# Two-layer decoder on one core: the causal mask of the transposed scores moves from mask matmuls on TensorE to a GpSimd selection on the exponentials

## The reference, cut to what matters

```
qkv = x @ W_qkv;  q = layernorm(q, q_scale);  k = layernorm(k, k_scale)
scores = einsum("bshd,bthd->bhst", q / sqrt(8), k)
scores = where(future, finfo.min, scores)          # keys behind the query are left out
attn   = softmax(scores);  ctx = einsum("bhst,bthd->bshd", attn, v)
x = layernorm(x + ctx @ W_out)
```

## Time and profile before

| | |
|---|---|
| three runs | 491.47, 491.82, 494.59 us; median 491.82 |
| profiled execution | 493.74 us, its span in the trace 491.9 us |
| PE | 458.1 us busy, 93% |
| DVE | 384.5 us, 78% |
| ACT | 351.2 us, 71% |
| POOL | 190.2 us, 39% |
| mean granted clock of TensorE | 0.984 |

### The profile page before, as it was taken

The page is one execution under the profiler, slowest core; times in us unless marked ns, Lnnn a source line. Parts: engine busy times, 40 slices in busy tenths (PEclk is TensorE's granted clock), DMA queues, the critical chain, the costliest instruction groups (busy, mean ns, idle before and its releaser), DMA issues.

```text
span 491.9 us, 12390 instructions
## 1 busy us (share of the span) xinstructions
PE 458.1 (93%) x4416; PEld 307.2 (62%) x4416; DVE 384.5 (78%) x1133; ACT 351.2 (71%) x893; POOL 190.2 (39%) x365
## 2 busy tenths in 40 slices
PE   5567989998999999999999999999999999999994
PEld 2344557655546546666778555658754756996894
DVE  3559998799899999997788888858788678554465
ACT  3326676866858769887776688986767878969743
POOL 8760001570101644344143232334414537646352
PEclk9689999999999999999999999999999999999999
DMA  7650310032300213001110000030000000000001
GB/s 240 152 148 4 105 31 25 4 86 73 88 4 23 66 39 85 17 2 26 35 35 21 6 3 2 4 88 4 2 13 13 0 2 1 1 2 1 1 1 43
DMA packets 27185, 18.40 MB, mean 37 GB/s; under 512 B 8217, under 2 KB 26773, under 8 KB 26997
## 3 DMA queue, kind: packets, MB, share of 16 engines
q1 hardware_dynamic: 23413, 15.44, 11.8%
q10 hardware_dynamic: 3712, 2.17, 1.7%
HBM read 5.58 MB, written 1.05 MB: 13 GB/s over the span
## 4 chain that ended last, share of the span: by engine, by line
PE 74%; DVE 9%; POOL 6%; issue 3%; ACT 3%; DMA 2%; SPq 2%; ACTq 0%; POOLq 0%; DVEq 0%
PE psum L1051 11%; PE psum L1372 6%; PE psum L1162 6%; PE psum L1395 6%; PE psum L1308 6%; PE psum L1103 5%; PE psum L1130 4%; DVE nmax L1788 4%; PE psum L1406 4%; PE psum L1152 3%; PE psum L1149 3%; PE psum L1417 2%; PE psum L1190 2%; PE psum L1082 2%; PE psum L1109 1%
## 5 line engine op out<-in xcount | busy, mean ns | idle before, releaser
L1537 ACT ACTIVATE EX<-psum 128x1024 f32<-128x1024 f32 (+1 forms) x128 | 118.5, 976 | 8.7 <-PE psum L1136 4.3
L1788 DVE TENSOR_REDUCE nmax<-psum 128x2 f32<-128x768 f32 (+1 forms) x96 | 77.5, 861 | 7.4 <-PE psum L1109 7.2
L1783 DVE TENSOR_REDUCE nmax<-psum 128x4 f32<-128x616 f32 (+1 forms) x80 | 68.1, 876 | 2.9 <-PE psum L1103 2.6
L1103 PE MATMUL psum<-K,Q 64*128 64x154 bf16 (+4 forms) x512 | 50.9, 268 | 5.9 <-issue 4.5
L1014 POOL TENSOR_TENSOR GP<-REST,xrs 128x512 f32<-128x512 f32 (+1 forms) x48 | 32.5, 700 | 41.4 <-DVE xrs L2025 27.6
L1130 PE MATMUL psum<-Q,K 64*128 64x512 bf16 (+3 forms) x320 | 44.7, 315 | 1.6 <-DVE nmax L1788 1.2
L1620 ACT ACTIVATE REST<-psum,nxmax 128x154 f32<-128x154 f32 x96 | 36.2, 395 | 10.7 <-DVE nxmax L2015 9.8
L1444 ACT COPY pvraw<-psum 128x512 f32<-128x512 f32 x32 | 18.7, 585 | 34.3 <-PE psum L1162 24.6
L1103 PEld LDWEIGHTS psum<-K,Q 64*128 64x128 bf16 x512 | 21.4, 95 | 28.2 <-issue 19.1
L1162 PE MATMUL psum<-EX,V 128*32 128x256 f32 (+3 forms) x512 | 37.8, 435 | 0.1
L945 POOL TENSOR_SCALAR rstd_rest<-moments_rest 128x2 f32<-128x2 f32 x32 | 7.3, 228 | 79.1 <-DVE moments_rest L1831 78.7
(11 more groups left out here) (338 smaller groups left out, 1162.4 us busy)
## 6 DMA issues: line engine op xcount, KB each, us to landing
Q<-xparts SPq DMA_DIRECT2D x24, 128.0 KB
Q<-parts SPq DMA_DIRECT2D x21, 128.0 KB
K<-parts SPq DMA_DIRECT2D x21, 128.0 KB
X<-in_x SPq DMA_DIRECT2D x4, 256.0 KB, 3.6
Q<-in_L_xattn_Wkv SPq DMA_DIRECT2D x1, 1024.0 KB, 6.6
K<-xkparts SPq DMA_DIRECT2D x24, 38.5 KB
out<-XB_rest SPq DMA_DIRECT2D x6, 128.0 KB, 1.9
Q<-in_L_xattn_Wq SPq DMA_DIRECT2D x1, 512.0 KB, 4.4
```

The costliest lines, as they stand in the source:

```text
L1103: last = mm(to[:, r, at:at + n], Q6[a][p, b % 2, 2 * g + jj, P * q:P * q + P], K6[a][p, b % 2, 2 * g + jj, 0:n], start=True, stop=bool(a))
L1537: drains(nc.scalar.activation(dst, src, ACT.Exp), key)
L1783: last = vec.tensor_reduce(nmax[:, :, :, q], src[:, :, 0:2 * n].rearrange("p r (j k) -> p r j k", j=2), AX.X, ALU.max, negate=True)
L1788: last = vec.tensor_reduce(nmax[:, :, jj, q], src[:, :, at:at + P * (q + 1)], AX.X, ALU.max, negate=True)
```

## The change

`maskT` and its four mask matmuls for each piece go; `EX` is written by ACT as before, and POOL then sets to zero, in place, what lies behind the query: `diagonal`, one `affine_select` of 128 x 2 x 128 for each of the eight pieces of a self turn. It waits until ACT has written the unit, and "PV" of a self turn waits for a new semaphore, `ex_masked`, instead of ACT's last exponentials. In the setup, POOL no longer makes `maskT`: two selections of 64 x 256 and one `tensor_scalar` of 128 x 256 fewer. `MERGE` and `BANK_OF` are new tables of the same length: the same steps in another order.

```diff
@@ MERGE and BANK_OF: new tables, first line of MERGE of each
-    "rrrrrrwurrrrwllrlruuurrlrsssssuuuuvsssusuttsstrrttsssspptssttttllpsssrpptsslltttstpu"
+    "rrrrrruwurrurrlwlrrrrrrullsssssuuuusssssttsurltvttsssspptsstptttlsssrsppllttsstttpuu"
...
+        ex_masked = sem("ex_masked")
...
-        maskT = sb("maskT", [P, 2, P], BF16)
...
-            def masked(dst, keep):
...
-            step(masked(maskT, -1))
-            masked(maskS, 1).then_inc(consts_ready, 1)
+            for r in R:
+                p = slice(TILE * r, TILE * r + TILE)
+                step(nc.gpsimd.affine_select(out=halves_of[p, :, :], in_=ones_of[p, :, :],
+                                             compare_op=ALU.is_ge, fill=0.0, base=0,
+                                             pattern=[[TILE, 2], [-1, P]], channel_multiplier=1))
+            nc.gpsimd.tensor_scalar(maskS[:, :, :], halves_of, -1.0, -MASKED, ALU.add, ALU.mult
+                                    ).then_inc(consts_ready, 1)
...
+            def diagonal(b, a, g, u):
+
+                if a:
+                    return
+                drained(pool, (b, "ST", 0, g, u))
+                first = ex_slot(b, 0, g, u)
+                for at, jj, k in SELF_T_PIECES[u]:
+                    block_ = EX[:, first:first + 2, at:at + P]
+                    last = nc.gpsimd.affine_select(out=block_, in_=block_, compare_op=ALU.is_ge,
+                                                   fill=0.0, base=0, pattern=[[0, 2], [1, P]],
+                                                   channel_multiplier=-1)
+                last.then_inc(ex_masked, 1)
...
-                    "spread": spread_v, "residual": residual}
+                    "spread": spread_v, "residual": residual, "ST": diagonal}
...
-                                  Q6[a][p, b % 2, 2 * g + jj, P * k:S], start=True, stop=bool(a))
-                    for e in (() if a else R):
-
-                        for r in R:
-                            p = slice(TILE * r, TILE * r + TILE)
-                            last = mm(to[:, r, at:at + TILE * (e + 1)], ident2[p, e, :],
-                                      maskT[p, e, 0:TILE * (e + 1)], start=False, stop=e == 1)
+                                  Q6[a][p, b % 2, 2 * g + jj, P * k:S], start=True, stop=True)
...
-                drained(pe, (b, "ST", a, g, T_UNITS[a] - 1))
+                if a:
+                    drained(pe, (b, "ST", a, g, T_UNITS[a] - 1))
+                else:
+                    pe.wait_ge(ex_masked, T_UNITS[0] * (NQ * b + g + 1))
```

More of the change, by code:

```diff
@@ new lines @@
+    "sswssppttststtpuusssspptsupstftttfususwsusfssrpptusffssurrttrrrttspcskfrptpstccprctt"
+    "tkkklxsssssppsttsstststrssspplplttplssfttfstsspptssfwppswssptfptsttssfctpptsssspppst"
+    "tpsrfcftttfsksksfssptspk01vts00sxst0rrrr1ttrrs0spc0ppc1sttttprt100ss0r1ppt1tpt0l1tt0"
+    "1sss001pp0ssss0010s1ttt0p10sss110pssf1p10fttt00sfl1p0l00l11ssppf10s0p00sf1f00tt11w0s"
+    "0t1s11s11011scspp11sttt1p00s11sss1pp01pttsc00tsf1cwt0tf11xs0ssfsppss10001tt1110stts1"
+    "k00c0stskkk00p1101spp011s1tt0001kst01tt101v0psss01ppst00tkstsps0tt100ssk00ppsst1ptst"
@@ L347 @@
+    "sft0s11f0pps1stt00p11ssf0ppsttt1000010sp0f0pp01fftt1tp01001cc100pp011cp1css1111fss00"
+    "11sv0sss1t101stt11f0010sx11f0tss1pp1sts0t0p101s100s0spp1kk0ttst0s1110s11100ppp1ttt11"
+    "01p0pp10pf00f11010011kkf001k12312320k23110k20012302213001123001323020001113211122101"
+    "0020031112231103331030022331132kk3kk213kkk322330222133322223131220333322222333233002"
+    "231233212322310333122200333"
 )
 BANK_OF = (
-    "024613570246135062406234523046270460246250624064206245064206420624016247024602460123"
@@ L351 @@
[L351 to L356, removed]
@@ L357 @@
-    "426305126734063264023467301425670267401523670415236047152630415762304156723051467235"
-    "046712350647123560471236504271365041273560412735064127530614275306142753061427536102"
-    "7453671024536710245673102456731"
+    "024613570246135062406234520462040674204360436024604270462704620460123460246240624501"
+    "624062146052064523064204672601426501420164206145206420603567042601426046026452067420"
+    "641026740276407264063246304260745026450265240164210647206420567203464023670246120456"
+    "204267042530612340264724036240632450624506124016724036402374502647501236047602374506"
@@ L360 @@
+    "723406534201654201675204620463201456720467230146204216740236740264072364067452062450"
+    "624106723045620645230167420634501672406724061246302643206324506324062704623745026745"
+    "230652064523015674230154620754230167254301642710456216723406243016423067145263046210"
+    "462104567230476230462104230674152360234670152364705126374501632745106327451032761453"
+    "076124537061245370612453270614532706145273061457230614572036145720361457203614572360"
+    "4517234605172346051723460517234"
 )
```

2 lines of the change are left out of this document (removed).

## The result

The changed kernel takes 504.48 us (median of four runs, 503.13 to 507.55), the kernel before in the same session 493.2 us; the ratio is 1.0225 [1.019, 1.0259]. It is slower by 2.25%, outside the range.

What follows compares the result with a forecast made beforehand. PE was taken to bound the kernel from 66 us on, with DVE close behind. Terms -7.0 - 1.9 + 0.9 + 1.7 + 0.5 = -5.8 us took the 491.82 us median to 486.0 us; range 479.5 to 494.5.

Steps and rivals of the forecast that it cites:

- The new order: Whole kernel: no cost term of its own; after 300 us the stretch should only shift.
- The masks: PE, 60 to 300 us: removing the mask matmuls of 78 chain pieces at 0.09 us each gives -7.0 us.
- The selections: POOL, 128 at 0.40 us each: costs of +3.1 us, from PV's wait, POOL's queue and the port.
- Rival B: DVE and DMAs hold the pace, so PE's relief returns as waits, mostly until 220 us: 490.1 us, chance 0.22.
- POOL's queue: After the clearing of Q, which starts at T: selections delay normalisation and PV of (1,0,2), to T + 20.2; +1.7 us (0 to +4.7).
- The port: DVE's 128 small operations in self and cross turns wait for POOL's selections: +0.5 us (0 to +2.5).
- Setup: Before the first scores: fewer POOL constants and setup transposes moved off the chain, -1.9 us (-3.5 to 0).
- Wait of PV: Self turns: PV waits for the last unit's two selections, delaying the ring EX: +0.9 us (0 to +2.7).
- Rival C: POOL's in-order queue becomes the bound at 0.80 us a selection, deciding from about 0.6: about 504 us, chance 0.12.
- The signs of being wrong: Selections over 0.6 us, PE waiting for POOL over 6 us in total, or length after 300 us changing over 2 us.
- rival A: PE's queue gives back nearly all and the new order hides the selections: 479.5 us, chance 0.14.

Runs made afterwards that it cites:

- Experiment 4: Changed kernel under the old tables, without any selections or mask matmuls, transposed scores left unmasked: 491.11 us, 0.9953 to the kernel before.
- experiment 1: Kernel before, mask matmuls kept on PE, with the new MERGE and BANK_OF tables alone: 501.87 us, 1.0175 to the kernel before.
- experiment 7: Kernel before with the new tables, except letters 132 to 470 (about 85 to 210 us) and their banks, kept old: 496.09 us, 1.0048.
- experiments 2: Changed kernel, POOL selections kept, with the old MERGE and BANK_OF tables: 535.94 us, 1.0871 to the kernel before.
- 11: Changed kernel with the new tables, except letters 132 to 470 and their banks, kept old: 524.8 us, 1.0637 to the kernel before.
- Experiment 5: Changed kernel with its selections made on a constant into an unread spare tile, each waiting for the one before, PV for exponentials alone: 502.58 us, 1.0179.
- experiment 10: Changed kernel without the selections of turns (0,0,2) and (3,0,2), where POOL has pauses: 505.62 us, 1.026 to the kernel before.
- experiment 6: Changed kernel with the DVE cast L1753 written as a maximum over an axis of one: 508.21 us, 1.0291 to the kernel before.
- experiment 9: Changed kernel without the selections of turns (1,0,2) and (2,0,2), which stand right behind a normalisation: 502.27 us, 1.0163 to the kernel before.

## Why the prediction was wrong

Two steps failed, and a third was too small. The new order was put at nothing and costs 8.6 us. The masks were put at -7.0 us, and with `maskT` in the setup they gave 4.8 under the new tables and 2.3 under the old ones. The selections were put at +3.1 us and cost 7.3. Together: 8.6 - 4.8 + 7.3 = 11.1 us, and 504.48 - 493.2 = 11.3 were measured.

**The masks, -7.0 us: a length on the chain taken for a gain.** I took the 78 pieces of the chain at their full length each. Experiment 4 gives 2.3 us in the old order, in which the pieces were counted. A piece's place on the chain says that PE was last there, not by how much: PE was busy 99% of 140 to 220 us, but DVE 94%, and with PE relieved DVE ends last more often (21% of the chain instead of 9%). Rival B said this and had 2.9 us for it; the row that spoke for it was in the prediction, and I gave B only 0.22. B's own time, 490.1 us, is as wrong, since it has no term for the order either.

**The order: no term at all, the largest miss.** The prediction costs the new tables only where they hide something. They cost 1.75% by themselves (experiment 1), 1.27% of that between letters 132 and 470 (experiment 7). They are also the price of the selections: under the old tables these cost 1.0871 - 0.9953 = 9.2% instead of 1.5% (experiments 2 and 4, and 11 for the one stretch). The new order keeps POOL's waits for exponentials away from its normalisations, and in the stretch PE is idle 7.7 us instead of 2.8. Which steps within these letters cost it, and whether an order with less idle time exists, was not tried.

**POOL's queue, +1.7 us (to 4.7): right in one place, the other left out.** At (1,0,2) the changed kernel has T + 19.7, and against the kernel without selections the turn is 113.77 - 111.57 = 2.2 us late. Of that, 0.3 was there at the start; 1.1 came because the normalisation has the seven selections ahead of it, so that its transposes on PE (L1058) start later; and 0.7 is PE's wait right before the product. By (2,0) 1.6 us are left. The same pattern of a normalisation with a turn's eight selections behind it stands at 173 us, and there the loss is 3.5 + 1.6 us, by the held cast and the clock. I followed POOL's queue only behind the clearing.

**The port, +0.5 us (to 2.5): the wrong kind of term.** I took 128 small operations with a mean price. The cost was in a single large cast, 3.88 instead of 0.43 us, at the head of a chain of gates that PE was about to need. The small ones got a little longer in the mean, as predicted: L1800 and L1804 took 197 and 174 ns, their successors 214 and 189. And PE's idle time had a price of its own, the lower clock behind it (2.1 us on one product), which stands in no term.

**Setup, -1.9 us: right, but not kept.** The first scores start at 28.68 us, 3.0 us earlier than the 31.65 of the earlier trace rows. The first PV starts only 0.3 us earlier (table above), since in the changed kernel the clock is low for longer. Before it was 0.57 from 32 to 36 us and 1.00 in the other stretches from 28 to 48; now (columns as in the earlier trace rows):
```profile
28.00:32.00 4.00, 3.32 (x48) 2.49 (x48) 2.52 (x3) 0.00 (x0) 3.89 (x6) 0.50 0.82 212
32.00:36.00 4.00, 3.11 (x22) 2.73 (x18) 3.89 (x8) 2.16 (x4) 2.46 (x4) 0.73 0.25 70
...
40.00:44.00 4.00, 3.58 (x26) 2.56 (x26) 3.86 (x10) 2.99 (x5) 0.82 (x2) 0.62 0.00 0
```
and in between DVE has the same maxima to do. That the clock is the whole reason was not shown.

**Wait of PV, +0.9 us (to 2.7): not measured by itself.** Experiment 5 was meant to, but has its loss in another place. The changed kernel's trace has PE idle 0.15 us ahead of the product of (0,1) for a selection, and 0.74 us ahead of that of (1,2), as read above. What the later products cost through the ring EX stays open.

**Rival C** had the right sign and a time (504) near the measured one, but for a reason that did not happen: it needed 0.80 us a selection, and they take 0.42. Its threshold of 0.6 us was wrong, because it was worked out from 8.9 us gained, of which at most 4.8 came.

**The signs of being wrong did not show.** The selections took under 0.6 us, PE's waits that the trace puts down to POOL are 0.95 + 0.15 = 1.1 us in all (1.8 with the 0.74 us), and the stretch behind (3,3) kept its length. The forecast failed by 17 us all the same (-5.8 against +11.3), because no sign watched what the new order does before 300 us. Two sums of the prediction are also off: rival A's terms give 481.4 and not 479.5 us (without the 2 us of DVE they give 479.4), and root and normalisation end by its own terms at T + 16.8, not 16.5. Neither bears on the failure.

In sum: without selections the changed kernel is 0.8% slower than before, tables (+1.75%) against masks gone (-1.0% under these tables); the selections add 1.5%, almost all of it between 95 and 200 us. No complete kernel tried here beats the one before; what a free mask could bring under the old tables is the 0.5% of experiment 4. The stand-ins of experiment 5, each waiting for the one before, did not hold the cast; whether real selections spaced like that would not either was not tried.

## What to carry to other kernels

When an engine's queue is in the chain with a second engine over 90% busy beside it, price removed work by the second engine's room and not by its length on the chain alone (here 7.0 us on the chain were worth 2.3, with the second engine 94% busy). When work goes to an "idle" engine whose queue also holds steps that others need soon, walk that queue at every place where such a step stands, not only at the first: ask what waits behind each new wait, and what each new run of instructions stands ahead of. A new order is a term of its own, even where nothing seems wrong with it; run it alone with the old code, and give it a sign that would show it.

## What the runs showed of the hardware that was not expected

- A DVE operation can be held by POOL for much longer than one POOL instruction. The cast of 128x512 began with the first of eight selections and ended after all eight and one addition, 3.88 us instead of 0.43 (in the changed kernel and again in experiment 10); a subtraction with two SBUF inputs took 3.70 and 4.78 instead of 0.69 us (experiment 6). The Trainium skill, "SBUF — State Buffer", section "Who interferes with whom", names casts and operations with two SBUF inputs among those that can contend, and says that reductions never do on this chip; the traces agree on all three (the reduction took 0.69 us beside a busy POOL). It speaks of a block until the other instruction finishes; here it lasted over nine, one behind the other.
- Not every unbroken run of POOL does this. Beside the eight normalisations from 173.02 us, 6.23 us without a pause, DVE's small casts and subtractions took 0.30 to 0.39 us instead of 0.17, and beside the eight spaced selections of experiment 5 the subtraction took 1.02 us. The eight selections that held the cast took 2.93 us together, less than eight times their mean of 419 ns, so that they overlapped a little. Whether this overlap is what keeps DVE out was not shown.
- PE's granted clock was 0.50 for the 4 us from 186 us, after PE had been idle nearly all the time from 182 to 185.65 us, and the same 32 matmuls took 4.49 instead of 2.36 us. So this stall of 3.95 us cost another 2.1 us.
- Kernels with nearly the same work have different clocks at one place: 1.00 from 108 to 116 us in the changed kernel, but 0.76 and 0.82 in experiment 9, 0.74 and 0.83 in experiment 10, 0.77 and 0.80 in experiment 5. In experiment 10 all the selections there are in place, so it isn't the missing ones. The group of twelve matmuls that took 1.84 us in the changed kernel took 3.21 in experiment 9. A part of any single difference of 1 to 2 us between such kernels is this, and no run here separates it, nor whether it belongs to the kernel or to the one profiled execution.
